# Joining ScalarE's squares and two rectifications, and giving it nine scaled copies a layer in batch 0, in a fused embedding, interaction and MLP kernel

## The reference, cut to what matters

```python
e = jnp.stack([tbl_0[ids[:, 0]], ..., tbl_15[ids[:, 15]]], axis=1)      # (2048, 16, 256)
xk = x = e
for i in range(3):
    z = jnp.einsum('bfe,bge->bfge', x, xk).reshape(B_, F_ * F_, E_)
    z = jnp.swapaxes(z, 1, 2)
    z = jnp.einsum('bcl,oc->bol', z, Ws[i]) + bs[i][None, :, None]
    z = jax.nn.relu(z)
    z = jnp.sum(z, axis=-1)
    outs.append(z)
    xk = jnp.broadcast_to(z[:, :, None], (B_, F_, E_))
h = jnp.concatenate([outs..., dense_ctx], axis=1)
h = jnp.maximum(h @ W_top1 + b_top1, 0.0)
h = jnp.maximum(h @ W_top2 + b_top2, 0.0)
y = h @ W_top3
```

## Time and profile before

| what | value |
|---|---|
| median of 3 runs | 579.08 us (576.73 to 579.23) |
| profiled execution, its own time | 579.74 us |
| its span in the trace | 578.0 us |
| mean granted PE clock | 0.956 of full speed |
| PE, DVE, ACT, POOL busy | 476.3, 542.8, 498.7, 467.8 us |

### The profile page before, as it was taken

One profiled execution on the slowest core, in us unless ns is written; L12 is line 12 of the kernel. 1 busy time (PEld: TensorE's weight loads), 2 busy tenths in 40 slices (PEclk: granted clock), 3 DMA queues, 4 the chain that ended last, 5 costly groups with the idle time before them and its releaser, 6 DMA issues.

```text
span 578.0 us, 10773 instructions
## 1 busy us (share of the span) xinstructions
PE 476.3 (82%) x3990; PEld 190.8 (33%) x3990; DVE 542.8 (94%) x326; ACT 498.7 (86%) x1471; POOL 467.8 (81%) x354
## 2 busy tenths in 40 slices
PE   5559888687888798878989788798869888789988
PEld 5213233232333333232333323233333323233324
DVE  1697999999999999999999999999999999999994
ACT  1143698999999999999999999989999999999875
POOL 6665888889888888888888889888888888888630
PEclk9689898999989989998999999799999989999979
DMA  3352212221222122212221222212212212210000
GB/s 98 92 145 74 75 56 57 63 64 56 74 58 64 56 71 72 67 56 74 62 64 56 69 60 61 73 57 82 64 56 66 61 60 74 57 54 1 1 2 0
DMA packets 14334, 35.43 MB, mean 61 GB/s; under 512 B 5493, under 2 KB 5879, under 8 KB 14266
## 3 DMA queue, kind: packets, MB, share of 16 engines
q0 software_dynamic: 12288, 33.57, 20.3%
q1 hardware_dynamic: 1994, 1.17, 0.8%
HBM read 34.71 MB, written 0.01 MB: 60 GB/s over the span
## 4 chain that ended last, share of the span: by engine, by line
DVE 38%; ACT 28%; PE 18%; issue 10%; POOL 3%; another core or an unknown queue 1%; DMA 1%; ACTq 0%; DVEq 0%; POOLq 0%
DVE prod L436 32%; ACT outer L637 15%; PE z_ps L827 8%; DVE outer L485 6%; ACT outer L627 3%; ACT sq L582 3%; POOL x_rows L342 3%; PE t_ps L790 3%; ACT relu L593 2%; ACT xt L574 2%; PE turn_ps L898 1%; PE turn_ps L902 1%; PE turn_ps L860 1%; PE zs_ps L842 1%
## 5 line engine op out<-in xcount | busy, mean ns | idle before, releaser
L436 DVE TENSOR_TENSOR prod<-t_ps,xt 128x2048 f32<-128x2048 f32 x190 | 420.8, 2281 | 11.0 <-remote 6.7
L342 POOL DMA_INDIRECT x_rows<-in_tbl,ids_sb x256 | 248.4, 970 | 73.1 <-issue 62.0
L637 ACT ACTIVATE outer<-outer,bias_sb 128x256 f32<-128x256 f32 x476 | 236.7, 518 | 3.0 <-DVE outer L485 3.0
L827 PE MATMUL z_ps<-prod,w_sb 128*32 128x512 f32 x1520 | 191.2, 622 | 37.3 <-DVE prod L436 34.3
L356 POOL TENSOR_TENSOR intra<-xt 128x1024 f32<-128x1024 f32 (+4 forms) x90 | 205.1, 2281 | 6.0 <-PE z_ps L827 4.5
L574 ACT ACTIVATE xt<-t_ps 128x512 f32<-128x512 f32 x128 | 75.2, 604 | 45.2 <-PE t_ps L790 21.7
L637 ACT ACTIVATION_READ_ACCUMULATOR outer<-outer,bias_sb 128x1 f32 x476 | 100.2, 210 | 0.0
L485 DVE TENSOR_TENSOR outer<-y_ps,z_all 128x1408 f32<-128x1408 f32 (+2 forms) x60 | 93.4, 1598 | 4.5 <-ACT outer L627 3.5
L790 PE MATMUL t_ps<-ident,x_rows 128*128 128x128 f32 x512 | 81.2, 288 | 19.0 <-DMA x_rows<-in_tbl,ids_sb 7.1
L827 PEld LDWEIGHTS z_ps<-prod,w_sb 128*32 128x32 f32 x1520 | 45.8, 111 | 124.8 <-issue 93.3
L790 PEld LDWEIGHTS t_ps<-ident,x_rows 128*128 128x128 f32 x512 | 55.9, 143 | 81.8 <-issue 59.6
(11 more groups left out here) (69 smaller groups left out, 219.1 us busy)
## 6 DMA issues: line engine op xcount, KB each, us to landing
x_rows<-in_tbl,ids_sb POOLq DMA_INDIRECT x256
w_sb<-in_w SPq DMA_DIRECT2D x1, 512.0 KB
feat<-in_dense SPq DMA_DIRECT2D x1, 128.0 KB
w_sb<-in_w SPq DMA_DIRECT2D x1, 128.0 KB
ids_sb<-in_ids SPq DMA_DIRECT2D x1, 120.0 KB
ident<-in_identity SPq DMA_DIRECT2D x1, 64.0 KB, 2.1
w_sb<-in_w0t SPq DMA_DIRECT2D x1, 64.0 KB
sel_sb<-in_sel SPq DMA_DIRECT2D x1, 48.0 KB
```

The costliest lines, as they stand in the source:

```text
L342: pool.indirect_dma_start(out=x_rows[:, par, f, :], out_offset=None, in_=tables[f], in_offset=bass.IndirectOffsetOnAxis(ap=ids_sb[:, NF * ...
L436: dve.tensor_tensor(prod[:, m % PROD_RING, half, :].rearrange("p (f g s) -> p f g s", f=QF, g=QF), t_ps[:, tbank(b, q, half), :, :].unsque ...
L637: act.activation(outer_of(b)[:, o // OP, o % OP, :], outer_of(b)[:, o // OP, o % OP, :], ACT.Relu, bias=bias12_sb[:, layer - 1, o:o + 1], ...
L827: mm = pe.matmul(z_ps[j * GR:(j + 1) * GR, m % 2, 0:n], w0_sb[:, half, slot, :], src[:, half, j * n:(j + 1) * n], start=(slot == 0 and hal ...
```

## The change

It has these parts.

- `square` does both halves in one instruction of 4096 elements a partition, in place of two of 2048.
- `rectify_two(b, 1)` does pairs 1 and 2 of a batch in one instruction over both banks of `z_ps`, in place of `rectify(b, 1)` and `rectify(b, 2)`; it waits for `u4`, the last part of pair 2, and for the sum of pair 0. The last batch keeps its single ones.
- `rectify(b, 0)` stands ahead of `copy_tile(b, 3, 1)`.
- `copy_tile(b+1, 2, 0)` stands ahead of ACT's part of `mlp_c`.
- Batch 0 gets 9 slices on ACT in layer 1 and 9 in layer 2 (frame 1), so that DVE's pieces shrink from 8x176 and 8x160 to 8x112 elements.
- On PE `transpose_tile(b+1, 0, 0)` stands ahead of `mlp_a`, `contract(b, "sq")` ahead of `mlp_b`, and `sum_pairs(b, 0)` ahead of the transposes of group 1.

```diff
+FIRST_SLICES = {1: 9, 2: 9}
...
         def slices(b, layer):
 
+            if b == 0:
+                return FIRST_SLICES[layer]
             return SLICES[layer] if b < LAST - 1 else 0
...
-            def square(b, half):
-                if half == 0:
-                    act.wait_ge(copied, tile(b, 3, 1) + 1)
-                    if b > 0:
-                        act.wait_ge(contracted, part(b - 1, "sq") + 1)
-                act.activation(sq[:, half, :], xt[:, b % 2, half, :, :].rearrange("p f s -> p (f s)"),
-                               ACT.Square).then_inc(squared, 1)
+            def square(b):
+                act.wait_ge(copied, tile(b, 3, 1) + 1)
+                if b > 0:
+                    act.wait_ge(contracted, part(b - 1, "sq") + 1)
+                act.activation(sq[:, :, :].rearrange("p h n -> p (h n)"),
+                               xt[:, b % 2, :, :, :].rearrange("p h f s -> p (h f s)"), ACT.Square).then_inc(squared, 1)
...
+            def rectify_two(b, k):
+
+                m = pair_no(b, k + 1)
+                act.wait_ge(contracted, part(b, pairs_of(b)[k + 1][-1]) + 1)
+                if m >= 2:
+                    act.wait_ge(summed, m - 1)
+                act.activation(relu0[:, :, :], z_ps[:, :, :], ACT.Relu, bias=bias0_sb[:, :]).then_inc(rectified, 2)
...
                 slice_outer(b - 1, 1)
+                rectify(b, 0)
                 copy_tile(b, 3, 1)
-                rectify(b, 0)
                 move_feat(b - 2)
-                square(b, 0)
-                square(b, 1)
+                square(b)
...
                 slice_outer(b - 1, 2)
-                rectify(b, 1)
-                rectify(b, 2)
+                rectify_two(b, 1)
                 copy_tile(b + 1, 1, 0)
                 copy_tile(b + 1, 1, 1)
...
                 rectify(b, 3)
+                copy_tile(b + 1, 2, 0)
                 mlp_in(frame, "mlp_c")
-                copy_tile(b + 1, 2, 0)
...
                 contract(b, "u2")
+                transpose_tile(b + 1, 0, 0)
                 mlp_in(frame, "mlp_a")
-                transpose_tile(b + 1, 0, 0)
+                contract(b, "sq")
                 mlp_in(frame, "mlp_b")
-                contract(b, "sq")
                 transpose_tile(b + 1, 0, 1)
                 contract(b, "u3")
                 form_yt(b)
                 contract(b, "u4")
+                sum_pairs(b, 0)
                 transpose_tile(b + 1, 1, 0)
                 transpose_tile(b + 1, 1, 1)
-                sum_pairs(b, 0)
                 sum_pairs(b, 1)
```

More of the change, by code:

```diff
@@ L732, in _ @@
             move_z0(LAST - 1)
-            square(LAST, 0)
-            square(LAST, 1)
+            square(LAST)
             mlp_in(LAST, "mlp_a")
@@ L812, in contract @@
                 elif name == "sq":
-                    pe.wait_ge(squared, HALVES * (b + 1))
+                    pe.wait_ge(squared, b + 1)
                     src = sq
```

## The result

The changed kernel took 584.45 us, median of 6 runs (582.64 to 587.92), the kernel before 579.13 on the same chip (6 runs, 576.73 to 579.61). The ratio is 1.0109, interval 1.0076 to 1.0143, so it is 1.1% slower. The ratio is not the quotient of the two medians, which differ by 5.3 us (0.9%). The forecast was 576.9, with 0.08 on slower. The profiled execution took 583.75 us; its span is 582.0, against 578.0 before.

The account below looks back on a forecast made before the run. POOL was taken to bound the middle, with DVE 8.7 us behind it. Gains of 1.2 + 0.9 + 0.1 = 2.2 us off the profiled 579.74 gave 577.5, against the median 576.9; range 573.5 to 579.6.

Parts of the forecast that it names:

- What bounds the kernel: Middle of the program: POOL has no slack from 122.97 to 518 us; DVE's outer product follows it by about 8.7 us.
- Frame 0 and DVE's start: Frame 0: earlier sum of pair 0 lets copies begin at about 53.6, DVE at 54.1, 1.1 us earlier (0.5 to 1.6).
- Rectification of pairs 1 and 2 in one: ACT, each batch: joining saves 0.10 to 0.19 us, taken as 0.15, and moves two waits; pair 1's bank frees later.
- What becomes of the 3.0 us: Frames 0 to 2: DVE gains 1.1 + 1.9 = 3.0 us; POOL's batch 3 comes only 0.3 earlier, at about 122.7.
- 1.45 of lateness to give back: POOL's waits of 0.64 at 88.38 and 0.81 at 122.97 absorb its start being some 1.1 us later.
- Nine slices: Batch 0: more ACT slices shorten DVE's pieces, saving 1.07 us in layer 1 and 0.80 in layer 2, 1.9 together.
- Fits barely: Batch 0: ACT's nine slices end at 67.5, DVE's piece was due at 68.43; both come about 1 us earlier.
- Squares, two in one: ACT, each batch: a joined instruction saves 0.10 to 0.19 us, taken as 0.15; 31 times, 4.6 us, 0.3 a frame.
- Frames 4 to 11, 12 to 14: Frames 4 to 11 gain 1.2 us (0.6 to 1.7) under POOL's limit; 12 to 14 gain 0.9 (nothing to 1.7).
- The joint rectification costs more than it saves: Rival: pair 1's bank frees about 0.4 us later, PE waits, its clock falls in eight more frames; 581.8 us, chance 0.08.

Follow-up runs that it names:

- e4: The kernel before with 24 POOL memsets of 0.205 us ahead of batch 3's first inner product; 585.02 us, ratio 1.011.
- e9: The changed kernel again, unaltered, on a chip with a quicker start; 569.88 us, ratio 1.0018 to the kernel before.
- e12: The changed kernel with pairs 1 and 2 rectified one by one, e1 again on a chip with a quicker start; 567.84 us, ratio 0.9978.
- e1: The changed kernel with pairs 1 and 2 rectified one by one, all else as changed; 577.54 us, ratio 0.999.
- e2: The changed kernel with five and six slices in batch 0 as before, in place of nine and nine; 581.21 us, ratio 1.0061.
- e3: The kernel before with only the joint rectification and the sum of pair 0 ahead of the transposes; 581.91 us, ratio 1.0046.
- e14: The changed kernel with 60 extra PE transposes ahead of u4 of batch 0; 588.14 us, ratio 1.0124.
- e16: The changed kernel with five and six slices in batch 0 and 60 extra PE transposes ahead of u4 of batch 0; 588.63 us, ratio 1.0126.
- e15: The changed kernel with pairs 1 and 2 rectified one by one and 60 extra PE transposes ahead of u4 of batch 0; 585.96 us, ratio 1.0104.
- e13: The kernel before with 60 extra PE transposes ahead of u4 of batch 0; 590.95 us, ratio 1.0114.
- e11: The changed kernel with the joint rectification only from batch 2 on, separate ones in batches 0 and 1; 569.59 us, ratio 0.9994.
- e10: The changed kernel with the joint rectification in batches 0 and 1 alone, separate ones from batch 2 on; 568.95 us, ratio 1.0002.
- e7: The changed kernel with pairs 1 and 2 rectified one by one and five and six slices in batch 0; 567.78 us, ratio 0.9977.

## Why the prediction was wrong, step by step

**What bounds the kernel.** Right. POOL ran without a wait for PE from batch 3 to 521; e4 showed that a delay ahead of batch 3 arrives at DVE's last batch, 6.2 of 6.45 us. How it arrives can be seen in frame 6. The prediction had DVE's outer product at least 8.7 us behind POOL's last inner product of the batch, and so it comes, in batch 5 of the changed kernel:

```profile
225.40 1.28 POOL L359 TENSOR_TENSOR intra<-xt 128x512 f32<-128x512 f32 x1
```

```profile
235.35 3.15 DVE L488 TENSOR_TENSOR outer<-y_ps,z_all 128x1408 f32<-128x1408 f32 x2 [0.92 <-ACT outer L637]
```

POOL's product ends at 226.68, and DVE starts 8.67 later; in e4, e9 and e12 it is 8.68 or 8.69, and in the kernel before it is never below 9.5 where POOL made the whole batch. Until there DVE was 2.4 us late (123.9 against 121.5 at batch 3's units), behind it 4.1 (256.7 against 252.6 at batch 7's).

**Frame 0 and DVE's start.** Wrong, and this is the step that failed first: the joint rectification was to end at 53.6 and DVE to start at 54.1; they came at 56.17 and 56.79. The prediction's own sum does not give 53.6 either: 54.61, less 0.5 to 1.1, and 0.41 more for the longer instruction is 53.9 to 54.5. The prediction laid ACT's wait of 4.41 us to the eight transposes ahead of the sum of pair 0. The move of the sum did not shorten it. "Reported" means here that the semaphore came, read from the end of ACT's wait; by its rows PE had ended the sum earlier, at 52.6 before. The sum reported done at 53.94 before, at 54.32 in e1, 54.20 in e2, 55.05 in the changed kernel and 55.30 in e3, on the same kind of chip, ahead of the transposes in the last four (and behind them at 54.44 in e4). Something else holds PE until 54 to 55 us there (last section). The transposes were the nearest thing in the row, and no more.

**Rectification of pairs 1 and 2 in one.** The chain behind it was seen and sized rightly: from the end of the joint rectification to POOL's start the prediction had 3.8 (0.4 + 1.9 + 1.5), and it was 59.94 - 56.17 = 3.77. Its beginning was wrong, 53.6 against 56.17, and so POOL's start, 57.4 against 59.94. What the prediction did not see is what separate rectifications do with the hold-up. From the report of the sum of pair 0 to that of `i0`, PE needs 4.75 us in all five kernels with the joint one in which DVE is not waited for (the changed one, e2, e3, e14, e16), since everything is in a row: rectification, sum, `u5`, `i0`. With separate ones it is 2.37 (before), 2.70 (e1), 3.15 (e4): pair 1's rectification was done 5 us earlier, so the sum and `u5` went on without ACT. In e15, without a late report, it is 4.39, and the two forms differ by 0.36, close to the prediction's 0.4. So: 0.36 as a rule, nothing where DVE is waited for (e9), and 1.5 to 2.4 where reports come late (in e13, late and separate, it is 3.22).

**What becomes of the 3.0 us**, "the step that decides". The sentence that fell is that POOL's waits of 0.64 and 0.81 were "1.45 of lateness to give back". POOL waits there for `i0` of the batch before, and `i0` waits for the copies, rectifications and DVE pieces that started later too. In e2 and e3 POOL was 2.64 and 3.74 us later at batch 1, and the waits stayed at 0.64 and 0.8. All but 0.4 us of it was there at batch 3, 2.27 and 3.34: from one to the other it is 66.5 us before, 66.15 in e2, 66.12 in e3. So batch 3, forecast at 122.7, came at 127.61.

**Nine slices.** "Fits barely" was half right. DVE waited 0.91 at the first outer product:

```profile
70.97 2.09 DVE L488 TENSOR_TENSOR outer<-y_ps,z_all 128x896 f32<-128x896 f32 x2 [0.91 <-ACT outer L637]
```

DVE's gain stood: two pieces of 896 take 2.09, where two of 1408 took 3.15, so 1.06, against 1.07 in the prediction. The cost was on PE. ACT has nine slices of layer 2 ahead of the rectification in frame 1, and PE waits 1.9 to 3.1 us for it; in e2 and e16, with six, 0.99. In seven of the eleven kernels with nine slices PE's granted clock then fell to 0.50 of full speed, 1.2 GHz, over `u5`; in the other four it stayed at full, and in the seven with five and six slices it never fell there. A stretch of the changed kernel follows, and its `u5`. The row of the stretch has its length, the busy time of PE, of the weight loads, of DVE, ACT and POOL, each with the number of instructions, then PE's granted clock, the share of DMA and its GB/s.

```profile
86.00:95.00 9.00, 6.22 (x63) 2.57 (x64) 9.00 (x8) 7.59 (x20) 5.63 (x5) 0.81 0.20 60
```

```profile
88.78 0.66 PE L849 MATMUL zs_ps<-relu,sel_sb 128*32 128x128 f32 x8 [3.08 <-ACT relu L604]
89.21 3.11 PE L834 MATMUL z_ps<-prod,w_sb 128*32 128x512 f32 x16
92.14 1.46 PE L834 MATMUL z_ps<-intra,w_sb 128*32 128x384 f32 x16
```

and in e11 and e12, whose lists are the same up to there:

```profile
77.01 3.20 PE L838 MATMUL z_ps<-prod,w_sb 128*32 128x512 f32 x16
```

```profile
76.95 1.90 PE L835 MATMUL z_ps<-prod,w_sb 128*32 128x512 f32 x16
```

`u5` costs 1.1 to 1.3 more, and POOL's batch 2 came at 82.08 in e11 and at 80.83 in e12. e9 and e10 are such a pair too: 82.43 with the clock at 0.50, 80.85 with it at full. That the same list does both shows that it is partly chance. It came only behind waits of 1.9 to 3.1 us, never behind those of 0.99, and not behind all of the long ones. The Trainium skill, "TensorE: Matmul & The Clock Gate", section "Part 1: The HAM clock gate", has the clock set by how busy PE has been recently. The trace agrees in seven kernels; four with waits as long show no fall.

**Squares, two in one.** Mis-sized: from start to the next start a joined square takes 63.92 - 60.39 = 3.53 (e12), where two took 3.60: 0.07 saved, not 0.15. Two single rectifications in a row take 77.08 - 75.95 = 1.13 (e12), the joint one 56.17 - 55.15 = 1.02, others 1.00: 0.11 to 0.14 saved, against 0.15.

**Frames 4 to 11, 12 to 14.** The lead of 3.0 us that these steps were to spend was never there, so they were not tested as stated. The parts other than the joint rectification bring 1.3 us by the ratios of e7 and e12, of the 2.2 forecast, and that is not surely more than nothing.

**The rivals.** "The joint rectification costs more than it saves" named the part and the sign. Its mechanism, more frames at the lower clock, explains the smaller part at most: between 130 and 520 us the clock was at 0.50 for 17.1 us after and for 20.5 before, so there was not more of it, and PE's longer waits (24.3 us) are there without it too, 20.0 in e1. But the low stretches of frames 13 and 14 stand right behind waits for the joint rectification, and behind the first DVE waits 2.3 us, where e2 and e9 at full clock have 0.62. The larger part was paid ahead of POOL's batch 3. Of the 4.64 us there, 3.49 arose at batch 1, where e2 and e3 have 2.64 and 3.74, and separate ones 0.70 (e1) and 1.28 (e4): the joint rectification, with a hold-up that itself varies by 1 us. Nine slices and the clock made it 5.41 at batch 2; of these 1.92 us, 0.77 went into the wait ahead of batch 3, which the DVE pieces made shorter by the nine slices had turned into slack.

What is settled: the joint rectification makes the difference (e1 against the changed kernel; e3), the delay of POOL's early batches carries the larger part to DVE's last batch (e4), and on other chips there is hardly a loss (e9). Not settled is why the reports are late on two of four chips; whether the loss would vanish there without that, since no run can turn it off; and how much the low clock of frames 13 and 14 costs as a rule, since it is read in one execution. Two steps of the prediction failed, then: the end of the joint rectification at 53.6, which was 56.17, and the 1.45 us of POOL's waits taken for a reserve, which stayed. The version without joint rectification (e1, e7, e12) is the best of all: 0.999, 0.9977, 0.9978, not surely faster than the kernel before.

## What to carry to other kernels

Joining two instructions joins their waits: list for each of the two what it waited for and when that was there, since the earlier one's followers now wait for the later one's condition. Before a short wait on the bounding engine is counted as a reserve, ask whether its releaser moves with it. And where a wait is put down to an instruction in front of which others stand, look whether that instruction was really kept by them; here it was kept by something that an edit of the order could not touch.

## What the runs showed of the hardware

**Hold-ups in the first 55 us, on some chips.** On the chips where the kernel before takes 579 or 580 us, ACT, DVE and POOL resume together at 19.6 to 20.4 us, and ACT and POOL twice more between 30 and 49 us, from waits put down to "remote". In e1, and then the same instructions of DVE and ACT in e12:

```profile
19.79 4.49 DVE L439 TENSOR_TENSOR prod<-t_ps,xt 128x2048 f32<-128x2048 f32 x2 [6.62 <-remote]
```

```profile
19.84 0.60 ACT L577 ACTIVATE xt<-t_ps 128x512 f32<-128x512 f32 x1 [8.61 <-remote]
```

```profile
15.59 4.49 DVE L439 TENSOR_TENSOR prod<-t_ps,xt 128x2048 f32<-128x2048 f32 x2 [2.48 <-PE t_ps L798]
```

```profile
16.02 0.60 ACT L577 ACTIVATE xt<-t_ps 128x512 f32<-128x512 f32 x1 [4.85 <-PE t_ps L798]
```

By its rows PE had ended its transposes at 16.0 to 16.1 in both. The whole start costs some 8 us more. PE itself is held too: in e13 transposes that wait for nothing are issued one in 0.7 us, where later 53 of them take 7.48.

```profile
49.69 0.27 PE L986 MATMUL zs_ps<-ident 128*128 128x128 f32 x1 [0.47 <-issue]
50.41 0.32 PE L986 MATMUL zs_ps<-ident 128*128 128x128 f32 x1 [0.45 <-issue]
51.09 0.27 PE L986 MATMUL zs_ps<-ident 128*128 128x128 f32 x1 [0.36 <-issue]
...
53.89 7.48 PE L986 MATMUL zs_ps<-ident 128*128 128x128 f32 x53 [0.43 <-issue]
```

The cause is open.

**DVE and POOL on SBUF.** DVE's three shared inner products, with both inputs in SBUF, took 1.89 us before and 3.57 in the changed kernel, where they fell beside a POOL product:

```profile
86.17 3.57 DVE L466 TENSOR_TENSOR intra<-xt 128x768 f32<-128x768 f32 x3
```

```profile
86.70 1.28 POOL L359 TENSOR_TENSOR intra<-xt 128x512 f32<-128x512 f32 x1
```

That is 1.68 us for a product of 1.28. Of the same kind are the 3.24 to 3.26 us of e9 to e12. DVE's products with one input in PSUM keep a mean of 2.28 us, with POOL at work beside them all the time. The Trainium skill, "GPSIMD Engine Reference", section "1. Specifications", says that the two engines share their SBUF interfaces, with contention when a DVE instruction has two SBUF inputs. The trace agrees; the prediction had no term for it.
